# Second graph layer of a GNN and MoE program: the 24 sums of tile edges read saved rows instead of gathering them again

## What is computed

```
h_src = h_hc[src]
r_uv = r_hc[edge_type]
m = clifford_linear(h_src * r_uv, msg_w, msg_b)
gate = jax.nn.sigmoid(r_uv.reshape(r_uv.shape[0], -1) @ gate_w.T + gate_b)
m = m * gate[:, :, None]
...
h_agg = jax.ops.segment_sum(m, dst, num_segments=num_nodes)
```

## Times and profile before

| | |
|---|---|
| timed runs | 3772.03, 3770.55, 3781.87 us, median 3772.03 |
| profiled execution | 3753.33 us, its span 3751.6 us |
| granted clock of TensorE over the span, mean | 0.802 |
| busy over the span | PE 2350.0 us, PEld 1748.4, DVE 1677.4, ACT 1449.8, POOL 1986.0 |
| the stage of `aggregate` | 1974.4 us (first record of PE) to 3194.3 us (end of the last addition) |

### The profile page before, as it was taken

The page is one execution under the profiler, slowest core; times in us unless marked ns, Lnnn a source line. Parts: engine busy times, 40 slices in busy tenths (PEclk is TensorE's granted clock), DMA queues, the critical chain, the costliest instruction groups (busy, mean ns, idle before and its releaser), DMA issues. The chain is left out here.

```text
span 3751.6 us, 47569 instructions
## 1 busy us (share of the span) xinstructions
PE 2350.0 (63%) x11533; PEld 1748.4 (47%) x11533; DVE 1677.4 (45%) x4536; ACT 1449.8 (39%) x3766; POOL 1986.0 (53%) x1945
## 2 busy tenths in 40 slices
PE   1667767775786763777504554644554645679997
PEld 1245544544554543666402333423333433569996
DVE  5666555644555454000264544645554645531010
ACT  0354444533344332222244433423433433345553
POOL 2436544455555646655436767776777776023332
PEclk9988888887898875899856767766776766789998
DMA  6535544455565655556526666756665765254232
GB/s 225 196 112 171 152 133 139 143 155 175 179 193 181 204 156 188 177 165 184 175 77 202 191 173 176 206 167 180 196 193 164 206 175 154 87 189 120 59 81 60
DMA packets 366567, 605.79 MB, mean 161 GB/s; under 512 B 82338, under 2 KB 235179, under 8 KB 363536
## 3 DMA queue, kind: packets, MB, share of 16 engines
q1 hardware_dynamic: 261984, 331.36, 27.5%
q0 software_dynamic: 100208, 265.56, 26.3%
q10 hardware_dynamic: 4144, 6.20, 0.4%
HBM read 443.45 MB, written 164.32 MB: 162 GB/s over the span
## 5 line engine op out<-in xcount | busy, mean ns | idle before, releaser
L659 POOL DMA_INDIRECT agg_r_rows<-h_table,parts_and_x x832 | 863.9, 1038 | 390.6 <-issue 237.7
L715 PE MATMUL agg_r_sums<-agg_r_rows,agg_r_onehot 128*128 128x257 f32 x1664 | 590.8, 499 | 591.0 <-DVE agg_r_rows L697 310.0
L715 PEld LDWEIGHTS agg_r_sums<-agg_r_rows,agg_r_onehot 128*128 128x128 f32 x1664 | 375.6, 245 | 794.0 <-issue 559.2
L688 DVE TENSOR_TENSOR acc<-acc,agg_r_sums 128x257 f32 (+1 forms) x836 | 353.7, 423 | 523.1 <-remote 315.4
L626 ACT ACTIVATE agg_r_gap<-iota,parts_and_x 128x128 f32<-128x128 f32 x832 | 286.4, 392 | 608.2 <-remote 314.0
L1556 POOL DMA_INDIRECT rl_buf<-r_table,kinds x312 | 330.0, 1058 | 342.5 <-DMA relation_rows<-rl_buf 252.6
L1386 PE MATMUL la_acc<-la_parts,la_counts 128*128 128x512 f32 x1250 | 335.2, 425 | 102.5 <-ACT la_counts L1426 40.8
L1556 POOL DMA_INDIRECT rm_buf<-r_table,kinds x280 | 270.7, 967 | 223.7 <-DMA relation_rows<-rm_buf 118.5
L1956 PE MATMUL f_pH<-f_xT,f_w 128*128 128x128 f32 x2816 | 353.2, 283 | 49.4 <-DMA f_w<-in_L_ffn_w 19.5
L1956 PEld LDWEIGHTS f_pH<-f_xT,f_w 128*128 128x128 f32 x2816 | 337.7, 197 | 82.3 <-issue 50.5
L1975 PE MATMUL f_pY<-f_w,f_hT 128*128 128x256 f32 x1408 | 328.9, 383 | 22.3 <-DMA f_w<-in_L_ffn_w 11.3
(11 more groups left out here) (404 smaller groups left out, 3366.5 us busy)
## 6 DMA issues: line engine op xcount, KB each, us to landing
agg_r_rel<-relation_rows SPq DMA_DIRECT2D x404, 260.0 KB
relation_rows<-rl_buf SPq DMA_DIRECT2D x156, 260.0 KB
relation_rows<-rm_buf SPq DMA_DIRECT2D x140, 260.0 KB
relation_rows<-f_rr_buf POOLq DMA_DIRECT2D x60, 260.0 KB
f_w<-in_L_ffn_W SPq DMA_DIRECT2D x28, 512.0 KB
f_w<-in_L_ffn_W SPq DMA_DIRECT2D x14, 1024.0 KB
agg_r_rows<-h_table,parts_and_x POOLq DMA_INDIRECT x832
f_w<-in_L_ffn_w SPq DMA_DIRECT2D x38, 256.0 KB
```

What stands on the lines that cost most here:

```text
L659: pool.indirect_dma_start(rows[:, n % SLOTS, t, :], None, table, bass.IndirectOffsetOnAxis(ap=indices[:, t:t + 1], axis=0)).then_inc(s_row ...
L688: v.tensor_tensor(here, here, sums[:, (2 * (n - LAG) + t) % BANKS, 0:used], ALU.add).then_inc(s_acc, 1)
L715: last = nc.tensor.matmul(sums[:, (2 * n + t) % BANKS, 0:used], onehot[:, n % HOT, t, :], rows[:, n % SLOTS, t, 0:used], start=True, stop= ...
```

## The change

- `b_start` now holds the number of the half instead of its first row.
- `xn` becomes `saved`, with 26 slots of 257 columns, one for each tile (the last is for halves past the end).
- ScalarE copies each of the 808 multiplied halves to the slot of its tile (`keep`). The copy of block n - 2 lies around the Relu of block n. Each copy loads the tile's number from `b_tile` into a register and waits for the copy before it. Since halves come in order, a slot keeps the last half that starts in its tile, which is the one that the next tile shares.
- TensorE waits for the copies of a block (`s_save`) in place of the product (`s_ready`). For the 12 extra blocks it loads for each half the number of the half and with it the tile's number (`again`), and takes the rows from `saved`.
- SyncE, GpSimd and VectorE stop loading, gathering and multiplying after block 404.

```diff
@@ edge_blocks
-                sp.dma_start(c.tab["b_start_d"], at[:, 0, :]).then_inc(s_saved, 16)
+                sp.dma_start(c.tab["b_start_d"], at[:, 1, :]).then_inc(s_saved, 16)
@@ aggregate, scalar
+                def keep(half):
+                    at = half + 2 * LAG
+                    tile = act.value_load(c.tab["b_tile"][0:1, at:at + 1], min_val=0, max_val=NT)
+                    n, t = divmod(half, 2)
+                    act.wait_ge(s_ready, n + 1)
+                    if half:
+                        act.wait_ge(s_save, half)
+                    nc.scalar.activation(saved[:, bass.ds(tile, 1), :].rearrange("p a d -> p (a d)"), rows[:, n % SLOTS, t, 0:used], ACT.Copy)\
+                        .then_inc(s_save, 1)
                 def places(n):
-                    g = n
+                    g, older = n, n - BEHIND
                     act.wait_ge(s_sum, g + (SLOTS + 2 - HOT))
                     for t in range(2):
                         last = nc.scalar.activation(gap[:, n % HOT, t, :], c.iota[:, 0:P], ACT.Abs, bias=c.tab["b_near"][:, bass.ds(g * 2 + t, 1)])
                     last.then_inc(s_gap, 1)
+                    if 0 <= older < BLOCKS:
+                        keep(2 * older)
                     act.wait_ge(s_gap, g + 1)
                     nc.scalar.activation(onehot[:, n % HOT, :, :], gap[:, n % HOT, :, :], ACT.Relu, bias=1.0, scale=-1.0).then_inc(s_oh, 1)
+                    if 0 <= older < BLOCKS:
+                        keep(2 * older + 1)
@@ aggregate, sync
-                for n in range(BLOCKS, total):
-                    starts = [sp.value_load(c.tab["b_start"][0:1, at:at + 1], min_val=0, max_val=EDGE_TILES * P)
-                              for at in (2 * (n - BLOCKS), 2 * (n - BLOCKS) + 1)]
-                    sp.wait_ge(s_sum, n + 2)
-                    for t in range(2):
-                        sp.dma_start(rel[:, n % SLOTS, t, :], relation_rows[bass.ds(starts[t], P), :]).then_inc(s_rel[n % SLOTS], 16)
@@ aggregate, gpsimd
-                for n in range(total):
+                for n in range(BLOCKS):
                     gather(n, c.tab["b_src"][:, n * 2:n * 2 + 2])
@@ aggregate, vector
                 for n in range(total):
-                    dve.wait_ge(s_rel[n % SLOTS], loads_of(n))
-                    dve.wait_ge(s_rows[n % SLOTS], (n // SLOTS + 1) * 32)
-                    here = rows[:, n % SLOTS, :, 0:used]
-                    v.tensor_tensor(here, here, rel[:, n % SLOTS, :, 0:used], ALU.mult).then_inc(s_ready, 1)
+                    if n < BLOCKS:
+                        dve.wait_ge(s_rel[n % SLOTS], (n // SLOTS + 1) * 16)
+                        dve.wait_ge(s_rows[n % SLOTS], (n // SLOTS + 1) * 32)
+                        here = rows[:, n % SLOTS, :, 0:used]
+                        v.tensor_tensor(here, here, rel[:, n % SLOTS, :, 0:used], ALU.mult).then_inc(s_ready, 1)
                     add(n)
@@ aggregate, tensor
-                def sum_up(g, n):
-                    pe.wait_ge(s_acc, 2 * (g + LAG + 1))
-                    pe.wait_ge(s_oh, g + 1)
-                    pe.wait_ge(s_ready, g + 1)
+                def again(n, t):
+                    at = 2 * (n - BLOCKS) + t
+                    half = pe.value_load(c.tab["b_start"][0:1, at:at + 1], min_val=0, max_val=HALVES - 1)
+                    tile = pe.value_load(c.tab["b_tile"][0:1, bass.ds(half + 2 * LAG, 1)], min_val=0, max_val=NT)
+                    return saved[:, bass.ds(tile, 1), :].rearrange("p a d -> p (a d)")
+                def sum_up(n):
+                    terms = [rows[:, n % SLOTS, t, 0:used] if n < BLOCKS else again(n, t) for t in range(2)]
+                    pe.wait_ge(s_acc, 2 * (n + LAG + 1))
+                    pe.wait_ge(s_oh, n + 1)
+                    pe.wait_ge(s_save, min(2 * n + 2, HALVES))
                     for t in range(2):
-                        last = nc.tensor.matmul(..., rows[:, n % SLOTS, t, 0:used], start=True, stop=True)
+                        last = nc.tensor.matmul(..., terms[t], start=True, stop=True)
                     last.then_inc(s_sum, 1)
```

More of the change, by code:

```diff
@@ L59 @@
 EVEN = PARTS // 16 * 16
-SLOTS, BANKS, LAG, HOT = 12, 6, 2, 6
+SLOTS, BANKS, LAG, HOT, BEHIND = 12, 6, 2, 6, 2
 HALVES, PER_HALF = 2 * BLOCKS, 2 * PER_PART
@@ L496, in _ @@
                 starts = c.tab["a_start"][0:1, P // SW:P // SW * EDGES_AT + 1:P // SW]
-                v.tensor_scalar(at[:, 0, :], starts, bits, bits, ALU.arith_shift_right, ALU.logical_shift_left)
                 v.tensor_scalar(at[:, 1, :], starts, bits, None, ALU.arith_shift_right)
@@ L603, in aggregate @@
     total = BLOCKS + EDGES_AT // 2
+    saved = c.saved[:, :].rearrange("p (t d) -> p t d", d=used)
     with Core(nc) as k:
@@ L611, in aggregate @@
         s_rows = [c.pool_sem(f"{name}_rows{s}") for s in range(SLOTS)]
-        s_gap, s_oh, s_ready, s_sum, s_acc, s_gate = (k.sem(f"{name}_{x}") for x in (
-            "gap", "onehot", "ready", "sum", "acc", "gate"))
+        s_gap, s_oh, s_ready, s_save, s_sum, s_acc, s_gate = (k.sem(f"{name}_{x}") for x in (
+            "gap", "onehot", "ready", "save", "sum", "acc", "gate"))
         with nc.Block() as block:
@@ L667, in _ @@
                 v = nc.vector
-                def loads_of(n):
-                    slot = [q for q in range(n + 1) if q % SLOTS == n % SLOTS]
-                    return sum(16 if q < BLOCKS else 32 for q in slot)
                 def tile_of(half):
@@ L708, in _ @@
                 last.then_inc(s_sum, SLOTS + 1)
-                def sum_up(g, n):
-                    pe.wait_ge(s_acc, 2 * (g + LAG + 1))
-                    pe.wait_ge(s_oh, g + 1)
-                    pe.wait_ge(s_ready, g + 1)
+                def again(n, t):
[8 more added lines that the diff above has]
+                    pe.wait_ge(s_save, min(2 * n + 2, HALVES))
                     for t in range(2):
-                        last = nc.tensor.matmul(sums[:, (2 * n + t) % BANKS, 0:used], onehot[:, n % HOT, t, :], rows[:, n % SLOTS, t, 0:used],
-                                                start=True, stop=True)
+                        last = nc.tensor.matmul(sums[:, (2 * n + t) % BANKS, 0:used], onehot[:, n % HOT, t, :], terms[t], start=True, stop=True)
                     last.then_inc(s_sum, 1)
                 for n in range(total):
-                    sum_up(n, n)
+                    sum_up(n)
                     beside.tensor(pe, n)
@@ L2596, in build @@
         crowded_gnn0(nc, c, I, edges, h_tables, x1, zh0)
-        c.xn = c.sb("xn", [P, NT, D])
+        c.saved = c.sb("xn", [P, (NT + 1) * (D + 1)])
+        c.xn = c.saved[:, 0:NT * D].rearrange("p (t d) -> p t d", d=D)
         logits = [c.sb(f"logits{q}", [P, NT, ne]) for q, ne in enumerate((E0, E1))]
```

## The result

| | before | after |
|---|---|---|
| median of the timed runs, us | 3771.29 (3767.47 to 3781.87, 4 runs) | 3869.22 (3862.93 to 3876.8, 4 runs) |
| ratio, 95% interval | 1 | 1.0277 (1.0235 to 1.0319) |
| span of the profiled execution, us | 3751.6 | 3868.3 |
| clock of TensorE, mean | 0.802 | 0.792 |
| instructions in the profile | 47569 | 52405 |

A forecast was written before the change was run, and what follows sets the result against it. GpSimd's chain of gathers was taken to bound the stage, with only 98 us belonging to the engines behind. From 3772.03 us, -30.6 + 31.7 + 1.4 = +2.5 gave 3774.5 us, range 3748 to 3825.

The forecast's parts named there:

- Gathers that go, -30.6: GpSimd's chain in the stage: without its last 24 of 832 gathers it ends 30.6 us earlier.
- it costs nothing in the steady state: ScalarE's block with copies, 1.67 us for 1.03, lies under the 2.52 us or more of two gathers.
- a catch-up: About 28 us after a late stretch in which engines behind GpSimd gain on it; forecast some 5 us longer.
- the sum: Whole kernel: -30.6 + 31.7 + 1.4 = +2.5 us; chance 0.38 of staying the same within 0.3%.
- once in 120: ScalarE's later register loads in the trace: one of up to 1314 ns among 120, median 282 ns.
- the late stretches: 14 stretches of about 30 us in the stage, one in about 83 us, where sums come late, cause unknown.
- The tail, 31.7 + 1.4: Stage's end: twelve extra blocks at 2.64 us cost 31.7 us; block 403's sum starts 1.4 us later.
- Their new pace is that of PE's sequencer: Extra blocks on TensorE: four register loads in order with checks, addresses and issue set 2.64 us a block.
- ScalarE can't catch up: Slower rival, after late stretches: ScalarE's block at 2.2 us adds 61 us (3833), at 2.1 some 12 (3784); chance 0.30.
- The page's floor: Slower rival: each new load takes 0.6 us, ScalarE's block 2.15 us, an extra block 3.9 us, 3815 us; chance 0.07.
- Chances: Whole kernel's outcome: faster 0.25, same 0.38, slower 0.37.

The follow-up runs named there:

- the idle waits: Changed kernel without register instructions on ScalarE, four idle waits in place of each copy's four: 1.0215 to the kernel before with slow instructions, 1.0058 without.
- the kernel with TensorE's idle waits: Kernel before the change with eight more idle waits a block on TensorE: 0.9988 and 0.999 without slow instructions, 1.0036 with them.
- the loads ahead: Changed kernel without checks on ScalarE, TensorE loading the 24 tile numbers of the extra sums early and unchecked: 0.9979 to the kernel before.
- fixed slots: Changed kernel with each copy going to slot half number modulo the tiles, so no register instructions on ScalarE: 1.0021 to the kernel before.

## Why the prediction was wrong

- **Gathers that go, -30.6.** Right: GpSimd's chain ends with the 808th gather.
- **"it costs nothing in the steady state."** This step failed: the 808 gathers took 102.3 us longer in the profile. The undisturbed durations held: ScalarE's block in a catch-up is 1.74 us for 1.67, TensorE's loads are 298 and 303 ns for 290, and the copies 0.42 us. What the sum left out is that the durations of instructions in a queue are not one distribution. I took medians (282, 310 ns) and passed over the maxima of 715 and 1314 ns beside them, of which I called the second "once in 120". In that trace 4 of those 120 loads of ScalarE are over 0.6 us, and 26 of VectorE's 812 take 0.68 to 0.72 us. The second group bears this mechanism's mark. In the late stretches, where I could not say why sums were late, ScalarE's block of 15 instructions takes not 1.67 but, as shown above, 7.8 us, and it stands between product and sum. All 15 at 0.70 us each would be 10.5 us. The sum had no term for this. The change in the two surroundings (1.0276 and 1.0076) and the idle waits (1.0215 and 1.0058) show it. The late stretches didn't become much more frequent: waits of over 5 us ahead of VectorE's additions are 45 for 43.
- **The tail, 31.7 + 1.4.** In size 41.1 us without slow instructions (2680.8 to 2727.0 less the 5.1 us between last gather and last sum in the kernel with TensorE's idle waits), 8 too little. An extra block is 3.19 us, not 2.64, as the timeline of the changed kernel without slow instructions shows:

```profile
2693.39 2.08 PE L729 MATMUL agg_r_sums<-xn,agg_r_onehot 128*128 x4 [1.12 <-DVE acc L693]
2696.57 2.08 PE L729 MATMUL agg_r_sums<-xn,agg_r_onehot 128*128 x4 [1.10 <-DVE acc L693]
```

The four loads with checks and addresses are about 2.0 us of it (2 x (298 + 151 + 18) + 2 x (303 + 2 x 98 + 18) ns). So I had the loads right (2.08 in the sum). The other 1.2 are what is left for the issue of eight matmul and weight instructions with the waits, which I had put at 51 ns each; how they divide isn't shown. "Their new pace is that of PE's sequencer" was right: with the loads ahead a block takes 1.0 us, though the profile puts the waits down to "DVE acc".
- **The rival "ScalarE can't catch up"** named the place (ScalarE between VectorE and TensorE, GpSimd's waits over 130 us, and 217 measured), and I gave it 0.30. Its mechanism was another: it wanted a catch-up of 2.1 us a block or more, and undisturbed that stayed 1.74. The loss arises in the disturbed stretches, not behind them.
- **The page's floor** of the Trainium skill (DMA: Bandwidth & Descriptors, section Latency and other measured facts), 600 ns a `tensor_load`, is not what happens: the medians are 274 and 277 ns in the two surroundings. Idle waits of 38 ns lost nearly the same. That rival was also mis-summed: if 2.1 us a block adds 12 us and 2.2 adds 61, then 2.15 adds 37 and not 25, which makes it 3827, just above the range.
- **Chances.** Without slow instructions the change costs 22.5 us by the medians (3296.52 for 3274.01), which is slower too; there a sum with 41.1 in place of 33.1, and 10.9 us of slower gathers (1069.6 us for 808, where the kernel with TensorE's idle waits has 1090.2 x 807/831 = 1058.7), gives 20.5 with the 31.5 us that the 24 gathers take there. So even without the disturbance +2.5 was too low by 18 us, 8 of it in the tail and most of the rest in the steady state.

What stays open: what makes the instructions slow. Fetches of 8 KB of instructions rise with their number (136 packets before, 172 after, 146 with fixed slots), one for about 135 of ScalarE's instructions. That would be some 46 for its 6216 in the stage, and there are 37 clusters (47 if only pauses of up to 4 us count as inside). But VectorE, with nine instructions a block, shows only a few (49 in the kernel before). And the changed kernel has the same 172 packets, 91 of them in the stage with a median of 309 ns, in both surroundings, so the fetches alone don't make the instructions slow. Whether the disturbance needs them, no run separates.

## What to carry to other kernels

Count the instructions that a change puts into the queue of an engine that stands between two others, whatever they do: register loads, checks, addresses and waits were five of the six for each copy, and four of them, not the copies, cost 2.6 of the 2.8 per cent among slow instructions. Read minimum and maximum beside the median, and look into the windows where "issue" fills a gap; a stretch of a trace that you can't explain should widen the price of everything that you add to it. Before costing an added helper, take it off the path (wait for the product, let the slot's release wait for the copy), leave out run-time checks, and load ahead what is known early: together that turned 1.0076 into 0.9954 in one surrounding and 1.0276 into 1.0036 in the other.

## What the runs showed of the hardware that I had not expected

The same kernel takes 3274 or about 3775 us from one set of runs to another. In the long kind, some instructions in ScalarE's, VectorE's or TensorE's queue take 0.70 us, or 1.40, whatever they are: a load of 0.28, a register operation of 0.15, a check of 0.018 or an idle wait of 0.038 us. On ScalarE they come in clusters, most of them 10 to 35 us long. In the short kind none of the 4065 on ScalarE does. GpSimd's waits for a slot without slow instructions, in the kernel with TensorE's idle waits, are 33.2 us, so about two thirds of the 98 us of the kernel before look to be of the same origin; before itself has no profile without them here.
